# Both halves of the down-projection behind the fifth round of a pass, in a pipelined transformer and expert kernel on one core

## The reference, cut to what matters

```
xn = ln(h, ln1)                                  # 256 x 128
q, k, v = xn @ Wq.T + bq, xn @ Wk.T + bk, ...    # 16 heads of 8
scores = (q.k + rel_shift((q + u).r)) * 8**-0.5  # causal, 256 x 256 a head
h = h + softmax(scores) @ v @ Wo.T + bo
fn = ln(h, ln2)
h = h + gelu(fn @ W1.T + b1) @ W2.T + b2         # 128 -> 512 -> 128
```

## Time and profile before

| | us |
|---|---|
| median of 3 runs | 2552.3 (2550.67 to 2555.22) |
| profiled execution, its time | 2553.8 |
| profiled execution, its span | 2551.8 |
| one pass in the steady stretch (first score load to the next pass's) | 16.40 |
| first scores, first and last load (128 passes) | 42.9 to 2150.5 |
| granted TensorE clock, mean | 0.994 |

### The profile page before, as it was taken

How to read it: one execution, slowest core, us unless ns; L and a number is a source line. 1 busy time by engine, 2 the same in 40 slices (tenths; PEclk the granted TensorE clock), 3 DMA queues, 4 the chain that set the end, 5 groups by cost and what they waited for, 6 DMA issues and landing times. The chain is left out here.

```text
span 2551.8 us, 80664 instructions
## 1 busy us (share of the span) xinstructions
PE 2417.8 (95%) x31360; PEld 1980.5 (78%) x31360; DVE 2075.5 (81%) x5069; ACT 1854.8 (73%) x2837; POOL 1172.9 (46%) x2091
## 2 busy tenths in 40 slices
PE   3899999999999999999999999999999999599998
PEld 2678787888888888888888888888888887477776
DVE  5898889888888888888888888888888885477775
ACT  2577777778777777878787777877787777455554
POOL 5445554545444444445444454454444442233332
PEclk9999999999999999999999999999999999799999
DMA  6222323223332333222333333222332231100000
GB/s 190 81 84 77 89 80 86 82 79 86 85 86 81 89 87 85 82 83 84 85 87 86 85 86 86 83 81 83 85 86 82 84 86 31 41 26 26 26 22 17
DMA packets 221129, 195.88 MB, mean 77 GB/s; under 512 B 28880, under 2 KB 217424, under 8 KB 220752
## 3 DMA queue, kind: packets, MB, share of 16 engines
q1 hardware_dynamic: 220752, 190.73, 26.6%
HBM read 14.46 MB, written 4.19 MB: 7 GB/s over the span
## 5 line engine op out<-in xcount | busy, mean ns | idle before, releaser
L818 DVE TENSOR_REDUCE rowmax<-bank 128x4 f32<-128x1024 f32 (+1 forms) x768 | 937.1, 1220 | 253.5 <-PE bank L466 253.5
L639 ACT ACTIVATE probs<-bank 128x1024 f32<-128x1024 f32 x768 | 786.6, 1024 | 394.3 <-PE bank L509 388.5
L466 PE MATMUL bank<-kstack,qstack 62*128 62x128 f32 (+1 forms) x4096 | 435.0, 305 | 0.0
L509 PE MATMUL bank<-qstack,kstack 64*128 64x256 f32 (+1 forms) x4096 | 432.5, 304 | 0.0
L678 ACT ACT_TABLE_LOAD x256 | 328.4, 1283 | 4.5
L466 PEld LDWEIGHTS bank<-kstack,qstack 62*128 62x128 f32 x4096 | 314.6, 193 | 0.0
L509 PEld LDWEIGHTS bank<-qstack,kstack 64*128 64x128 f32 x4096 | 312.6, 191 | 0.0
L455 PE MATMUL bank<-mask_half,pick_half 64*128 64x128 bf16 (+1 forms) x3072 | 268.8, 243 | 33.4 <-DVE rowmax L818 21.8
L528 PE MATMUL bank<-probs,v_pad 128*32 128x256 f32 x4096 | 275.0, 386 | 1.5 <-ACT probs L639 1.5
L588 PE MATMUL bank<-w,hidden 128*128 128x128 f32 x2048 | 271.1, 276 | 0.9 <-ACT hidden L687 0.9
L498 PE MATMUL bank<-maskT_half,pick_half 64*128 64x128 bf16 (+1 forms) x3072 | 268.7, 243 | 1.9 <-ACT probs L639 1.9
(11 more groups left out here) (144 smaller groups left out, 5306.5 us busy)
## 6 DMA issues: line engine op xcount, KB each, us to landing
qstack<-base SPq DMA_DIRECT2D x768, 128.0 KB, 2.4
kstack<-base SPq DMA_DIRECT2D x384, 128.0 KB, 2.4
turn_x<-turn_c SPq DMA_DIRECT2D x512, 32.0 KB, 1.9
qstack<-maxrows SPq DMA_DIRECT2D x256, 16.0 KB
xin<-in_x SPq DMA_DIRECT2D x16, 256.0 KB, 3.0
out<-ot SPq DMA_DIRECT2D x16, 256.0 KB, 2.4
h_all<-in_x SPq DMA_DIRECT2D x2, 512.0 KB, 5.4
w<-in_w SPq DMA_DIRECT2D x4, 256.0 KB, 3.8
```

Of the source, the lines that this page charges most:

```text
L466: last = pe.matmul(bank[:, b, i * wide:(i + 1) * wide], qstack[rows, r, p0 + i, t * 128:(t + 1) * 128], kstack[rows, r, p0 + i, 0:wide], s ...
L509: last = pe.matmul(bank[:, 2 + b, i * wide:(i + 1) * wide], kstack[rows, r, p0 + i, kt * 128:(kt + 1) * 128], qstack[rows, r, p0 + i, q0:S ...
L639: act.activation(probs[:, (ROUNDS * n + k) % PR], bank[:, 2:4, :], ACT.Exp, scale=SCALE).then_inc(exp_done, 1)
L818: dve.tensor_reduce(rowmax[:, t, :, p0:p0 + heads], bank[:, 0:2, :].rearrange("p b (h c) -> p b h c", h=heads), AX_X, ALU.max).then_inc(ma ...
```

## The change

In TensorE's loop, the call of the down-projection's half 0 leaves round 2 and stands in round 4, directly ahead of half 1. No instruction, wait or buffer is added or taken away, and no other engine's list changes.

```diff
                     if k == 2 and live(s - 5):
                         b4(s - 5)
-                    if k == 2 and live(s - 6):
-                        down(s - 6, 0)
                     if k == 3 and live(s - 4):
                         b1(s - 4)
                     if k == 3 and live(s + 1):
@@
                     if k == 4 and live(s - 4):
                         b2(s - 4)
                     if k == 4 and live(s - 6):
+                        down(s - 6, 0)
                         down(s - 6, 1)
```

## The result

The changed kernel takes 2667.8 us (median of 4 runs, 2667.37 to 2669.52) against 2553.1 of the kernel before: ratio 1.0451, 95% interval 1.0433 to 1.0469. Forecast were 2664 and a range of 2656 to 2676.

What follows compares the result with a forecast made beforehand. VectorE's row maximum was taken to open round 3 and TensorE's own work round 5, so the moved half costs 0.887 us in 124 passes: 2553.8 + 110.0 = 2663.8, forecast 2664 us, range 2656 to 2676.

Steps and rivals of the forecast that it cites:

- Round 2 gives nothing back: Round 2: VectorE's row maximum still opens round 3, so taking half 0 away gains 0; round 2 keeps 2.22 us.
- The half costs 0.89 in round 4: Round 4: TensorE's own work opens round 5, so eight added loads at 0.111 us cost 0.89 us a pass.
- The higher prices, 0.97 and 1.09: Upper prices of a half in round 4: its full row, or the load-kind switch paid twice; 2674 and 2689 us.
- The wait in front of round 3: TensorE's idle time before round 3, labelled "rowmax", grows from 0.15 to about 1.04 us a pass.
- All of it is passed on: Behind round 4: rounds 5 to 3 shift whole, so none of the 0.89 us is lost before the next round 4.
- 124 passes and ends that cancel: s = 6 to 129 give 110.0 us; gains in passes 128, 129 and costs in 130, 131 cancel within 1 us.
- Rival A: TensorE's total is the bound: round 2 shortens to 1.33, round 4 grows to 3.08, time stays 2554 us; chance 0.03.
- Rival B: Rounds 5 to 2: waits of rounds 1 and 4 vanish, loss 0.45 us a pass, time 2610 us; chance 0.03.
- Rival C: Idle before round 3 drops the clock to 1.2 GHz, round 3 doubles, another 238 us, 2902 us; chance 0.01.

Runs made afterwards that it cites:

- the cut of half 0: Kernel before with three of half 0's four down-projection matmuls left out in round 2: 2551.8 us, ratio 0.9997.
- key-product run: Kernel before with all three matmuls of the key product moved from round 5 to round 0, ahead of the value projection's: 2604.5 us, ratio 1.019.
- half 1 cut: Kernel before with three of half 1's four down-projection matmuls left out in round 4: 2514.7 us, ratio 0.9851.

## Why the prediction was right

- *Round 2 gives nothing back.* Right: 2.23 us before and after. Shown twice, by the cut of half 0 (0.9997) and by the half moved.
- *The half costs 0.89 in round 4.* Right; a steady pass measured 0.90. The loads took 1.87 for sixteen (1.86 in the earlier trace rows). The higher prices, 0.97 and 1.09, were not paid here; 1.09 is what a half costs where it is a group of its own.
- *The wait in front of round 3.* Forecast was 0.15 + 0.89 = 1.04 us; it is 1.10. The half ended 0.94 us behind the transposes ahead of it (1014.60 against 1013.46 + 0.20 in the earlier trace rows), and it is this stretch, not eight spacings of 0.111, that turned into idle time. The same holds for the sum of the waits: 117 us more (124 x 0.94), not 110. The time does not depend on it.
- *All of it is passed on.* Right in effect, and the reason given was incomplete. I wrote that round 5 is a solid block without a wait on VectorE. The key-product run shows that its first part hangs on ScalarE's exponential. That chain too starts at the opening of round 5, so it shifts whole, and the forecast stood. For taking work out of round 5 the same sentence gave a wrong answer.
- *124 passes and ends that cancel.* 110.0 us were forecast and 110.7 measured between first and last scores, with the gain of 0.3 in passes 128 and 129 as foreseen (round 2 from 2.19 to 1.90), and the passes with apply_0 lost the same 0.9 as the others. The other 3.3 us of the miss of 4 lie outside: 1.5 ahead of the first scores, where nothing had changed, and 1.8 behind the last. In the fourteen traces the first stretch takes 42.3 to 44.6 us and the last one 399.2 to 404.6, so neither can be told from their spread. So what the half costs in the draining passes is not shown. The prediction counted two of them, and half 0 stands in four, 130 to 133.
- *Rival A* (the total decides) is out by the result and by the cut. *Rival B* (part comes back): rounds 0, 1, 3 and 5 kept their length. *Rival C* (the clock): granted 0.994 before and after; round 2 of the changed kernel, with 1.10 us idle, has TensorE busy for 1.37 of 2.23 us at a clock of 1.00 (2.4 GHz):

```profile
1062.40:1064.63 2.23, 1.37 (x22) 0.95 (x18) 2.18 (x4) 1.77 (x3) 0.53 (x2) 1.00 0.11 29
```

The Trainium skill's rule of micro-idles that make the clock go back and forth ("TensorE: Matmul & The Clock Gate", A second HAM failure mode) is not borne out in this kernel with one gap of 1.10 us in each pass of 17.30.

## What to carry to other kernels

Where two engines hand a buffer to and fro, price a moved piece by the round it leaves and the round it enters: set the end of the releasing instruction beside the start of the released one in each. A gap of about 0.06 us means that the other engine opens the next round: the piece in front was free, and taking it out gains nothing (2551.8 against 2552.6 us here). It doesn't mean room for another: TensorE was almost level, and a half put into such a round cost 0.86 and 0.89 us. A longer gap means that a piece put in costs its full price, and that one taken out gains no more than the gap is longer than 0.06 (0.29 of 0.67 us with half 1 cut). A small idle time is no offer by itself: ask who waits for what stands in front of it. And a bound that explains a shift (all of round 5 moves) doesn't yet say what a cut there is worth.

## What the runs showed of the hardware that was not expected

- *The end of a group of weight loads costs about 0.2 us.* Behind a block of 32-column loads (line 535 in the kernel before) 0.20 us idle labelled "issue" stood in every kernel; a block of full-size f32 loads takes 0.31 us from its last load to the first of the mask or of the context, against a spacing of 0.111 inside. It is not so at every change: from the transposes to the down-projection (both full-size f32) the spacing stays 0.11, from the mask's loads to those of the scores it is 0.03 to 0.05, and from the up-projection's last load to the 32-column loads of line 476 it is 0.13. Joining pieces of one kind saves the 0.2; splitting one off adds it, as both runs with the half in round 1 show.
- *Two VectorE operations on SBUF changed length with the same operands.* A cast of 128 x 32 (line 827, now 826) went from a median of 314 to 696 ns, 38.2 to 85.7 us in all, and the norm's scaling (line 767, now 766) from 394 to 354 ns in the mean, 178.3 to 156.8 us. Their place beside GpSimd's work had shifted; that this is the cause was not tried. It cost nothing here: round 5, in which the cast stands, kept its 5.44 us.

```profile
L826 DVE CAST maxparts<-rowmax x128: 181/696/728, 59.0 to 2264.6; 128x32 fp32r<-128x32 f32 x128
```
